# Last stage's mixes begun by ScalarE at the eviction, and the token shift's row copies moved to ScalarE

## The reference

```python
def _token_shift(xn, prev_row):
    first = (prev_row - xn[:, 0])[:, None]
    rest = xn[:, :-1] - xn[:, 1:]
    return jnp.concatenate([first, rest], axis=1)
...
xn = _ln(x, ln1_w, ln1_b)
sx = _token_shift(xn, state[:, i1])
...            # five mixes of xn and sx, projections, the scan over tokens, group norm, gate, Wo
x = x + att * g @ Wo.T
xn2 = _ln(x, ln2_w, ln2_b)
sx2 = _token_shift(xn2, state[:, i0])
xk = xn2 + sx2 * ffn_maa_k
xr = xn2 + sx2 * ffn_maa_r
rr = jax.nn.sigmoid(xr @ ffn_Wr.T)
kk = jnp.square(jax.nn.relu(xk @ ffn_Wk.T))
x = x + rr * (kk @ ffn_Wv.T)
```

## Time and profile before

| | |
|---|---|
| median of 3 runs | 2381.81 us (2381.59 to 2382.89) |
| the profiled execution | 2377.0 us, its span 2375.0 us |
| granted TensorE clock, mean | 0.969 |
| PE busy | 2211.8 us (93%) |
| DVE busy | 2137.8 us (90%) |
| ACT busy | 1020.3 us (43%) |
| POOL busy | 600.2 us (25%) |

### The profile page before, as it was taken

One profiled execution on the slowest core, in us unless ns is written; L12 is line 12 of the kernel. 1 busy time (PEld: TensorE's weight loads), 2 busy tenths in 40 slices (PEclk: granted clock), 3 DMA queues, 4 the chain that ended last, 5 costly groups with the idle time before them and its releaser, 6 DMA issues. The chain is left out here.

```text
span 2375.0 us, 41883 instructions
## 1 busy us (share of the span) xinstructions
PE 2211.8 (93%) x14272; PEld 1528.4 (64%) x14272; DVE 2137.8 (90%) x5337; ACT 1020.3 (43%) x3265; POOL 600.2 (25%) x858
## 2 busy tenths in 40 slices
PE   4697999999999999999999999999999999999866
PEld 3374766767676676767667676766767676666533
DVE  1369999999999999999999999999999999999973
ACT  2535263544526254452635345363634536363101
POOL 1122214131222404122241412223141232314200
PEclk8798999999999999999999999999999999999977
DMA  7001001010010101001010100101010010100000
GB/s 263 21 10 31 1 11 39 1 48 2 10 39 11 39 1 49 2 10 39 11 39 1 49 1 15 35 11 39 1 49 1 19 31 10 39 2 28 1 18 9
DMA packets 48420, 61.61 MB, mean 26 GB/s; under 512 B 20209, under 2 KB 25969, under 8 KB 48209
## 3 DMA queue, kind: packets, MB, share of 16 engines
q1 hardware_dynamic: 48208, 58.93, 7.9%
HBM read 42.14 MB, written 16.78 MB: 25 GB/s over the span
## 5 line engine op out<-in xcount | busy, mean ns | idle before, releaser
L1149 DVE TENSOR_TENSOR_SCAN st<-ws,st 128x256 f32<-128x256 f32 x1024 | 653.6, 702 | 0.2
L846 ACT ACTIVATE probs_or_mixes<-probs_or_mixes,least 128x128 f32<-128x128 f32 x1024 | 396.9, 396 | 105.8 <-DVE least L1096 105.6
L1000 POOL COPY st<-s 128x8 f32<-128x8 f32 x256 | 67.0, 279 | 1097.6 <-issue 933.7
L1138 DVE TENSOR_TENSOR st<-bank_pair,kT 128x1016 f32<-128x1016 f32 x256 | 308.8, 1206 | 29.4 <-PE bank_pair L696 21.7
L1159 DVE TENSOR_TENSOR st<-st,rT 128x1024 f32<-128x1024 f32 x256 | 329.4, 1302 | 0.0
L1096 DVE CUSTOM_DVE_ANT_0 probs_or_mixes<-bank,nmask 128x128 f32<-128x128 f32 x1024 | 228.8, 285 | 66.2 <-POOL nmask L988 33.8
L1024 POOL TENSOR_TENSOR probs_or_mixes<-probs_or_mixes 128x512 f32<-128x512 f32 x160 | 200.0, 1278 | 133.2 <-DVE probs_or_mixes L1215 133.2
L1030 POOL TENSOR_TENSOR rstd<-rstd,mhalf 128x1 f32<-128x1 f32 x96 | 95.0, 989 | 416.0 <-DVE rstd L1180 416.0
L846 ACT ACTIVATION_READ_ACCUMULATOR probs_or_mixes<-probs_or_mixes,least 128x1 f32 x1024 | 199.1, 194 | 0.0
L696 PE MATMUL bank_pair<-v_hi,sel 32*128 32x256 f32 x1024 | 165.7, 333 | 12.5 <-DVE st L1138 12.3
L857 ACT ACTIVATE probs_or_mixes<-bank 128x512 f32<-128x512 f32 x256 | 141.7, 594 | 78.6 <-PE bank L571 74.3
(11 more groups left out here) (139 smaller groups left out, 4207.9 us busy)
## 6 DMA issues: line engine op xcount, KB each, us to landing
cin<-in_ctx SPq DMA_DIRECT2D x16, 512.0 KB, 3.7
xin<-in_x SPq DMA_DIRECT2D x16, 512.0 KB, 3.7
x<-xin SPq DMA_DIRECT2D x16, 512.0 KB, 4.0
keep<-x SPq DMA_DIRECT2D x16, 512.0 KB, 3.6
out<-keep SPq DMA_DIRECT2D x32, 256.0 KB, 2.0
wo<-in_wo SPq DMA_DIRECT2D x2, 1024.0 KB, 11.4
nmask<-in_mask SPq DMA_DIRECT2D x16, 128.0 KB, 3.9
wq<-in_wq SPq DMA_DIRECT2D x1, 1024.0 KB, 10.7
```

The costliest lines, as they stand in the source:

```text
L846: last = fn(pr[:, n % 4, j, :], pr[:, n % 4, j, :], ACT.Exp, bias=least[:, n, j:j + 1], scale=-1.0, accum_out=rsum[:, n, j:j + 1])
L1138: tt(dst, src, over(kv, DU, 1), ALU.mult).then_inc(outer.sem, 1)
L1149: last = nc.vector.tensor_tensor_scan(v, ws[:, c].rearrange("p b t -> p (b t)"), v, 0.0, ALU.mult, ALU.add)
```

## The change

The eviction of `turn_m` on ACT now makes three results from each half of a bank instead of one: `mnT` as before, and the unshifted part of both mixes, `xn2 * (1 - m)`, straight from PSUM. For that, DVE derives at the start scaled columns `ln2_mix`: the LayerNorm's weight and bias, each times `1 - m`, for both mixes. `shift2` on DVE then adds `m` times the shifted `mnT`; the subtraction is gone. All five row copies go from DVE to ACT, as steps `row0` (earlier in DVE's `key`), `row1`, `row2` and `keep_row`. The four tables of steps are written anew.

```diff
+        ln2_mix = sb("ln2_mix", [2, 2, NC])
...
+            def row0(g, _):
+
+                act.wait_ge(emptied[XB.of(("turn_c", 1))], XB.through(("turn_c", 1), g))
+                wait(act, row_kept.sem, row_kept.after(g, 0))
+                wait(act, rows_copied.sem, rows_copied.after(g, 0))
+                fn(prev[:], cT[:, :, :, 0:2], ACT.Copy).then_inc(rows_saved.sem, 1)
...
+            def row2(g, _):
+
+                act.wait_ge(row_kept.sem, row_kept.after(g, 1))
+                wait(act, row_moved.sem, row_moved.after(g + 1, 1) if known(g + 1) else 0)
+                hold(act, filled, g, through("ffn_v", NB - 1, back=1))
+                src = prev3 if known(g + 1) else prev2
+                fn(mnT[:, :, :, 0], src[:], ACT.Copy).then_inc(rows2.sem, 1)
...
                 ps, free = y_full(("turn_m", p), g, through("ffn_v", NB - 1, back=1))
                 for q in range(2):
                     c = 2 * p + q
-                    last = fn(mnT[:, c, :, 1:], halves(ps, q), ACT.Identity, bias=col("ln2_b", c),
-                              scale=col("ln2_w", c))
+                    fn(mnT[:, c, :, 1:], halves(ps, q), ACT.Identity, bias=col("ln2_b", c), scale=col("ln2_w", c))
+                    for k, dst in enumerate((xk, xr)):
+                        last = fn(dst[:, c], halves(ps, q), ACT.Identity, bias=ln2_mix[:, k, 1, c:c + 1],
+                                  scale=ln2_mix[:, k, 0, c:c + 1])
                 last.then_inc(free, 1)
...
-                tt(sx2, mnT[:, :, :, 0:L], mnT[:, :, :, 1:], ALU.subtract).then_inc(shifted2.sem, 1)
-                dve.wait_ge(shifted2.sem, shifted2.after(g, 1))
                 for dst, name, sig in ((xk, "mk", mixk), (xr, "mr", mixr)):
                     for c in range(NC):
-                        stt(out=dst[:, c], in0=sx2[:, c], scalar=col(name, c), in1=mnT[:, c, :, 1:],
+                        stt(out=dst[:, c], in0=mnT[:, c, :, 0:L], scalar=col(name, c), in1=dst[:, c],
                             op0=ALU.mult, op1=ALU.add).then_inc(sig.sem, 1)
...
+            for k, name in enumerate(("mk", "mr")):
+                o = COLS[name][0]
+                for m in range(2):
+                    last = ts(ln2_mix[:, k, m, :], cols[:, o:o + NC], -1.0, 1.0, ALU.mult, ALU.add)
+            last.then_inc(derived, 1)
+            dve.wait_ge(derived, 3)
+            for m, part in enumerate(("ln2_w", "ln2_b")):
+                v = COLS[part][0]
+                last = tt(ln2_mix[:, :, m, :], ln2_mix[:, :, m, :], over(cols[:, v:v + NC], 2, 1), ALU.mult)
+            last.then_inc(derived, 1)
```

Other moves are read from the tables. On PE `spread.14+2` goes from before `low_rank.2` to behind it, so between it and `proj_r.0`; `spread.5` goes from before `score.4` to between `score.4` and `score.6`; `project.1` goes ahead of `spread.10`; `reduce.3` and `spread.9` go ahead of `flip.1`; `low_rank.4` goes behind `mean.1`:

```diff
-low_rank.0+1 reduce.5+2 spread.13+2 turn_c.0 turn_c.1 mean.0+2 tdecay.0+1 spread.14+2 low_rank.2+1 proj_r.0+1
...
+spread.12+2 low_rank.0+1 reduce.5+2 turn_c.0 spread.13+2 mean.0+2 turn_c.1 tdecay.0+1 low_rank.2+1 spread.14+2
+proj_r.0+1 spread.15+2 decay.0+1 turn_x.0 proj_v.0+1 key.0 proj_k.0+1 reduce.6+2 spread.0+1 decay.1+1 turn_x.1
```

More of the change, by code:

```diff
@@ new lines @@
+proj_r.0+1 spread.15+2 decay.0+1 turn_x.0 proj_v.0+1 key.0 proj_k.0+1 reduce.6+2 spread.0+1 decay.1+1 turn_x.1
+reduce.7+2 spread.1+1 query.0 spread.2+1 mean.1+2 low_rank.4+1 var.0+2 proj_r.1+1 spread.3+1 score.0 query.1
+proj_g.0+1 rstd.0+2 rstd.1+2 proj_g.1+1 score.2 spread.4+1 reduce.0+1 value.0 turn_p.0 turn_p.1 turn_p.2 score.4
+spread.5+1 score.6 out.0+2 turn_p.3 spread.6+1 reduce.1+1 values.0 out.1+2 turn_p.4 score.8 spread.7+1 turn_p.5
+turn_p.6 proj_v.1+1 turn_p.7 turn_m.0+2 proj_k.1+1 score.10 flip.0 values.1 turn_p.8 score.12 share.0 turn_p.9
@@ L130 @@
+spread.8+1 reduce.2+1 turn_p.10 score.14 turn_p.11 project.0 turn_m.1+2 turn_p.12 turn_p.13 reduce.3+1 values.2
+spread.9+1 flip.1 turn_p.14 turn_p.15 share.1 values.3 ffn_k.0+2 project.1 spread.10+1 ffn_r.0+2 ffn_k.1+2
+spread.11+1 ffn_r.1+2 turn_n.0 turn_n.1 ffn_v.0+2 ffn_v.1+2 low.0 reduce.4+1
 """
 ACT_ORDER = """
-turn_c.0 turn_c.1 mean.0+2 tdecay.0+1 proj_r.0+1 proj_v.0+1 turn_x.0 decay.0+1 key.0 proj_k.0+1 decay.1+1 turn_x.1
-proj_r.1+1 query.0 mean.1+2 score.0 query.1 proj_g.0+1 proj_g.1+1 score.1 score.2 turn_p.0 turn_p.1 turn_p.2 score.3
@@ L135 @@
[L135 to L138, removed]
+turn_c.0 mean.0+2 turn_c.1 tdecay.0+1 proj_r.0+1 turn_x.0 decay.0+1 proj_v.0+1 key.0 proj_k.0+1 turn_x.1 keep_row.0+1
@@ new lines @@
+decay.1+1 query.0 mean.1+2 proj_r.1+1 score.0 query.1 score.1 proj_g.0+1 proj_g.1+1 score.2 turn_p.0 turn_p.1
+turn_p.2 score.3 score.4 turn_p.3 score.5 score.6 turn_p.4 row0.0 score.7 turn_p.5 score.8 turn_p.6 row2.0+2
+apply2.0+2 apply2.1+2 proj_v.1+1 turn_p.7 score.9 turn_m.0+2 proj_k.1+1 flip.0 score.10 turn_p.8 score.11 share.0
+score.12 turn_p.9 turn_p.10 score.13 turn_p.11 score.14 score.15 turn_m.1+2 turn_p.12 turn_p.13 flip.1 turn_p.14
+turn_p.15 apply0.0 share.1 apply0.1 ffn_k.0+2 ffn_r.0+2 apply1.0 apply1.1 row1.0 ffn_k.1+2 turn_n.0 ffn_r.1+2
@@ new lines @@
+outer.1+1 weigh.0+1 scan.1+1 mix.4+1 outer.2+1 var.0+2 weigh.1+1 score.0 outer.3+1 score.1 scan.2+1 groupnorm.0+2
+proj_g.0+1 scan.3+1 score.2 score.3 proj_g.1+1 outer.4+1 value.0 scan.4+1 score.4 score.5 weigh.2+1 outer.5+1
+weigh.3+1 score.6 score.7 out.0+2 scan.5+1 norm2.0+2 outer.6+1 out.1+2 score.8 norm2.1+2 score.9 readout.0+1 scan.6+1
+inverse.0 proj_v.1+1 weigh.4+1 weigh.5+1 outer.7+1 score.10 score.11 scan.7+1 score.12 score.13 weigh.6+1 gather.0
+outer.8+1 score.14 score.15 weigh.7+1 scan.8+1 inverse.1 project.0 norm0.0 shift2.0+2 gather.1 outer.9+1 scan.9+1
@@ L157 @@
+norm1.0 project.1 norm0.1 weigh.8+1 weigh.9+1 readout.1+1 outer.10+1 norm1.1 outer.11+1 scan.10+1 scan.11+1
+weigh.10+1 shift.0 weigh.11+1 ffn_v.0+2 ffn_v.1+2 outer.12+1 mix.0 mix.1 readout.2+1 outer.13+1 scan.12+1 mix.2
+outer.14+1 mix.3 weigh.12+1
 """
```

77 lines of the change are left out of this document (25 added, 52 removed).

## The result

| | before | changed |
|---|---|---|
| median, the two run side by side | 2379.59 us (2375.36 to 2383.27, 14 runs) | 2375.14 us (2371.84 to 2379.19, 14 runs) |
| ratio | | 0.9979, 95% interval 0.9971 to 0.9988 |
| profiled execution, its span | 2377.0, 2375.0 us | 2376.15, 2374.1 us |
| one period | 137.8 us | 137.5 us |

The changed kernel is 4.5 us faster; forecast were 17. The direction held, the size did not. The period, the time from one group to the next, fell by 0.3 us where 1.3 was forecast. The two profiled executions lie only 0.85 us apart.

What follows compares the result with a forecast made beforehand. PE's own work, 135.28 us, was taken as the floor of a 137.8 us period. 1.3 us less in 14 periods (-18.5), with +2.4 and -1.0 at the ends, summed to -17.1 us: 2365 us, range 2346 to 2388.

Steps and rivals of the forecast that it cites:

- the first reading: PE in one period: its busy 135.28 of 137.80 us is the floor, so at most 2.5 us idle can be gained.
- Moved: PE's five waits per period: the new order fills four, leaving 1.2 us of waits against 2.52, period to 136.5 us.
- turn_n, 0.8 forecast to 0.1: PE's wait at L615 for apply1.1: norm0.0 ahead of shift2 and project.1 ahead of a spread leave 0.1 us.
- gT, 0.4 to 0.1: PE's wait at L562 behind proj_g: three row copies leave DVE's queue ahead of groupnorm, 0.1 us left.
- L675, "wait gone": proj_r.0's 0.5 us wait for mix.2's bank: spread.14, 0.58 us, now stands between and fills it.
- L751, "gone": out.0's 0.6 us wait for score.4's bank: spread.5, 0.58 us, between score.4 and score.6 fills it.
- flip.0 on turn_m.0's bank, 0.2 to 0.5: New PE wait: flip.0 writes the bank turn_m.0 had, held by six ACT evictions, 0.2 to 0.5 us a period.
- L562 behind turn_p, 0.3: PE's 0.3 us wait behind turn_p: replaced by the new waits on ACT around turn_m, counted as 0.6 us together.
- ffn_v.0, 0.2: PE's ffn_v.0 wants both ffn_k squares; the second eviction now stands behind apply1.1 and a row copy on ACT: 0.2 us.
- The walk through the dense stretch: ACT around turn_m.0 and turn_m.1, busy 18.91 of 19.50 us: 0.6 us of new PE waits, bounds 0 and 3.9.
- the slow rival: ACT's dense stretch runs over, 3.9 us uncovered: +2.6 us a period, 2419.6 us in all; chance 0.15.
- The -1.0 for the stretch in which DVE sets the pace: From 2207.6 to 2309 us, before the end: DVE loses one subtraction and two small copies, 1.5 us, taken as -1.0.

## Why the prediction was right in direction and wrong in size

**The step that failed** is the first reading: "PE's own work, 135.28 us, is the floor of a period". With it falls the way in which *Moved* costs a spread put somewhere else: "0.58 again", as if its time came along unchanged. Beside low_rank.4 a spread takes nothing on other rows, 0.47 where half its rows are the same, and alone it takes 0.67 (the runs above). Of the 1.05 us a period that are missing (137.55 for 136.5), 0.4 to 0.6 are PE busy longer, and the rest are waits: 1.6 to 1.8 us instead of 1.2.

**The waits, one by one.**
- turn_n, 0.8 forecast to 0.1: right, and more (-1.00 per step). The causes named are at most a part: with either norm0.0 or project.1 put back the wait stays away, and 0.5 us of it was apply1.1 standing behind ffn_k.1 on ACT, a move that the forecast names only as a cost for ffn_v.0.
- gT, 0.4 to 0.1: right (-0.42). That it went because the row copies left DVE's queue was wrong: without them in the old order it was 0.4 still, and with them in the new order it was gone. It went with the order.
- L675, "wait gone": it is 0.22 for 0.51, but the two steps ahead of it take longer, and the distance fell by 0.12 only. The step is false in itself. spread.14 stood ahead of low_rank.2 before, so the same two steps lie before proj_r.0 in both orders, and exchanging them fills nothing. The wait ends with DVE's mix.2, and that one starts when DVE's scans ahead of it are done, at 1219.30 us without idle time behind the last of them.
- L751, "gone": 0.6 to 0.4, with a new wait of 0.4 on the same DVE line at L562. The same fault: spread.5 stood beside score.4 before too, 1.02 us for both then and 1.01 now.
- flip.0 on turn_m.0's bank, 0.2 to 0.5: 0.20, right. Yet taking the evictions away did not shorten the period, so this term was never an addition: what waits at flip.0 does not wait at score.12.
- L562 behind turn_p, 0.3, "replaced by the walk above": score.12 no longer waits 0.26 for ACT there, but turn_p.9 waits 0.28 for ACT and score.12 0.21 for DVE.
- ffn_v.0, 0.2: no such wait in the changed kernel; it comes with norm0.0 or project.1 put back (0.15). For 0.2 unseen: POOL's mix.3 (+0.35) and turn_p.8 to score.12 (+0.35).

**DVE.** The cut of 2.54 us was sized right (130.6 where 131.0 was said). As a gain by itself it is zero, as the code without evictions in the old order shows. It pays only in the new order, where putting it back costs 1.3 us a period and putting norm0.0 back 1.09. The reading "two engines are nearly full" took DVE's busy time for work. Scans (L1149) in the period of the earlier trace rows (ns shortest, median, longest):

```profile
L1149 DVE TENSOR_TENSOR_SCAN st<-ws,st x64: 630/664/1702, 1107.7 to 1240.5; 128x256 f32<-128x256 f32 x64
```

Five DVE records of that period, three of them scans, are together 4.0 us longer than the median of their kind, and DVE's idle 4.25 us come on top. What stretches these five no run shows.

**ACT.** 0.455 an eviction and 0.25 a copy were near enough (0.47 and 0.21). The walk through the dense stretch was right for flip.0 in the new order. For the old one the slow rival was right: 2.1 us of waits, 1.3% slower.

**The ends.** +2.4 at the last turn_m is exact, though 1.2 of it come back at ffn_k.0. The -1.0 for the stretch in which DVE sets the pace did not come; there it lost 1.5 us (3.7 earlier at its start, 2.2 at mean.0). The term left out the clock: 20.5 us of that stretch are at the lower level, 13.7 before. In the same order but for one entry, the run with low_rank.4 beside spread.2 has 17.1 and takes 116.2 us from low_rank.0 to mean.0, the changed kernel 119.2. These are single executions, and no run changes the clock alone, so the cause stays open.

Of the signs named as proof, the busy time of PE was the one that spoke: it was to stay at 135.3 or fall, and it rose. None of the rivals had that outcome.

## What to carry to other kernels

PE's busy time is a property of the order too, not of the work alone: before moving a small matmul step, look whether it runs beside its neighbour (interleaved rows, two steps in the time of one), and on which 32 rows each of them sits. Here two engines were busy above 95%, and unloading one gave nothing until the steps that wait were moved; so try the move and the unloading apart and together. A wait can cost more than itself: after one of 1.4 us look at the granted clock before you put the rest down to other waits. A bank held longer cost time only where the next step on its ring was close; rename the neighbour in the order before counting the eviction.
